# Spline stage of an eight-sublayer decoder on one core: tile scores by TensorE on transposed signs instead of by VectorE and GpSimd row by row

## The reference, cut to what matters

```
xn  = (x - mean) * rsqrt(var + eps) * gamma + beta            # 2048 x 512, second norm of xn0
sig = sign(mean(spline_slopes, -1))                            # 64 tiles x 8 features: each tile owns 8 of the 512
tile_sigs[a, 8a+j] = sig[a, j], zero elsewhere                 # 64 x 512
cluster_sigs = sign(mean of the 8 tile_sigs of a cluster)      # 8 x 512
best_cluster = argmax(sign(xn) @ cluster_sigs.T)
tile = argmax(sign(xn) @ tile_sigs.T inside best_cluster)
x_slice = the 8 features of xn that the chosen tile owns
mn, mx = min and max of x_slice over all tokens that chose this tile
u = clip((x_slice - mn) / (mx - mn + 1e-8), 0, 1 - 1e-6);  gi = int(u * 16)
delta = (bases[tile, j, gi] + slopes[tile, j, gi] * (u*16 - gi)) * output_scale[tile]
out[token, the 8 features of the tile] = delta, zero elsewhere; the sublayer returns xn0 + out
```

## Time and profile before

| | us |
|---|---|
| median of three runs | 1837.11 |
| the profiled execution, its own time | 1835.21 |
| its span in the trace | 1833.4 |
| busy: TensorE / VectorE / ScalarE / GpSimd | 1331.3 / 1511.1 / 869.8 / 556.4 |
| spline phase in the trace, first to last instruction | 620.0 to 767.1 |

### The profile page before, as it was taken

One profiled execution on the slowest core, in us unless ns is written; L12 is line 12 of the kernel. 1 busy time (PEld: TensorE's weight loads), 2 busy tenths in 40 slices (PEclk: granted clock), 3 DMA queues, 4 the chain that ended last, 5 costly groups with the idle time before them and its releaser, 6 DMA issues. The chain is left out here.

```text
span 1833.4 us, 23885 instructions
## 1 busy us (share of the span) xinstructions
PE 1331.3 (73%) x6398; PEld 990.5 (54%) x6398; DVE 1511.1 (82%) x3239; ACT 869.8 (47%) x1726; POOL 556.4 (30%) x573
## 2 busy tenths in 40 slices
PE   4799228886999417444474199069999899998888
PEld 2354114444888303134341188057888788877776
DVE  5999378985877698799759789797899898988885
ACT  3455356662333141154331143136888788843443
POOL 0000005443110141400005013302576666666651
PEclk8999669997999755766585599589999999999999
DMA  5010420000000400155201010223688788888985
GB/s 172 23 35 1 189 75 1 0 0 1 1 1 1 129 23 0 46 162 171 92 0 41 1 46 24 69 51 115 213 242 253 232 245 259 247 249 250 277 238 156
DMA packets 91355, 198.41 MB, mean 108 GB/s; under 512 B 14856, under 2 KB 24200, under 8 KB 90384
## 3 DMA queue, kind: packets, MB, share of 16 engines
q0 software_dynamic: 27120, 91.25, 18.0%
q1 hardware_dynamic: 64160, 106.34, 17.3%
HBM read 181.81 MB, written 15.73 MB: 108 GB/s over the span
## 5 line engine op out<-in xcount | busy, mean ns | idle before, releaser
L2229 POOL DMA_INDIRECT L3f_gd<-rows,idx x160 | 181.0, 1131 | 204.8 <-DVE L3f_gd L2458 180.8
L2229 POOL DMA_INDIRECT L3f_gu<-in_L_ffn_e_up,idx x160 | 167.1, 1045 | 71.3 <-issue 47.2
L2297 PE MATMUL L3f_o_ps<-L3f_euh,L3f_ath 128*128 128x512 f32 x352 | 145.4, 413 | 15.9 <-DVE L3f_atl L2439 15.9
L2285 PE MATMUL L3f_h_ps<-L3f_xh,L3f_edh 128*128 128x512 f32 (+1 forms) x384 | 144.6, 376 | 8.2 <-DVE L3f_xl L2444 8.2
L926 POOL TENSOR_TENSOR L0f_hq<-L0f_hid,magic 128x1408 bf16<-128x1408 f32 x16 | 45.2, 2824 | 338.9 <-DVE L0f_hid L997 338.9
L2285 PE MATMUL L3f_h_ps<-L3f_xl,L3f_edh 128*128 128x512 f32 (+1 forms) x384 | 144.2, 375 | 0.0
L2285 PE MATMUL L3f_h_ps<-L3f_xh,L3f_edl 128*128 128x512 f32 (+1 forms) x384 | 144.2, 375 | 0.0
L2269 PE MATMUL L3f_g_ps<-L3f_oh 128*128 128x128 f32 x704 | 97.5, 283 | 62.7 <-DVE L3f_oh L2426 62.7
L2297 PE MATMUL L3f_o_ps<-L3f_euh,L3f_atl 128*128 128x512 f32 x352 | 137.6, 391 | 0.0
L2297 PE MATMUL L3f_o_ps<-L3f_eul,L3f_ath 128*128 128x512 f32 x352 | 137.5, 391 | 0.0
L2269 PEld LDWEIGHTS L3f_g_ps<-L3f_oh 128*128 128x128 f32 x704 | 91.3, 194 | 73.3 <-issue 68.8
(11 more groups left out here) (526 smaller groups left out, 3702.3 us busy)
## 6 DMA issues: line engine op xcount, KB each, us to landing
L3f_eu<-in_L_ffn_e_up SPq DMA_DIRECT2D x96, 256.0 KB, 4.8
L3f_ed<-in_L_ffn_e_down SPq DMA_DIRECT2D x96, 256.0 KB, 4.5
L2x_ed<-in_L_ffn_e_down SPq DMA_DIRECT2D x32, 256.0 KB, 3.4
rows<-L2x_eo SPq DMA_DIRECT2D x32, 256.0 KB, 2.4
ternary_wgu<-in_L_ffn_w_gate_upT SPq DMA_DIRECT2D x4, 1408.0 KB, 10.4
X<-in_x SPq DMA_DIRECT2D x4, 1024.0 KB, 10.6
L0x_V<-in_ctxT SPq DMA_DIRECT2D x8, 512.0 KB, 3.8
L1f_C<-in_ctx SPq DMA_DIRECT2D x2, 2048.0 KB, 12.6
```

The costliest lines, as they stand in the source:

```text
L2229: pool.indirect_dma_start(buf[j % ND][:, :], None, table, bass.IndirectOffsetOnAxis(ap=idx[:, j:j + 1], axis=0)).then_inc(sem[j % ND], 16)
L2285: last = pe.matmul(h_ps[h][:, 0:cols], lhsT=w[h][:, c, :], rhs=x[:, c, 0:cols], start=(c == 0 and m == 0), stop=(c == DC - 1 and m == 2))
L2297: last = pe.matmul(o_ps[a][:, :], lhsT=w[h][:, a * P:(a + 1) * P], rhs=x[h][:, :], start=False, stop=False)
```

## The change

It touches the spline phase alone.

- **Norm.** VectorE makes `nm = -m * r2`, and ScalarE writes `XN = r2 * x + nm` (no gamma, no beta), 16 activations. VectorE's two instructions per tile are gone.
- **Signs.** TensorE transposes `XN`: per group of four token tiles and per 128 features, four 128 x 128 fp32 transposes into one PSUM buffer of two (`turn`). ScalarE takes the sign from PSUM, with gamma as scale and beta as bias, both now one value per partition, into bf16 (`signs`), one activation of 128 x 512 for each. In ScalarE's list a sign and a norm of the next group alternate.
- **Scores.** A bf16 table `sigs` (feature x 64 tiles, the sign at the owned features) is made by GpSimd (a memset and two `affine_select`) and VectorE (one product). TensorE multiplies the turned signs by it, 4 x 4 matmuls of 64 columns per group, accumulating in PSUM (`score`); those of a group stand in TensorE's list behind the first two turns of the next group.
- **Choice and gather** run in two halves of eight token tiles: the first half needs the scores of groups 0 and 1 only. VectorE reads the scores from PSUM. The gather multiplies `XN`, and its products are written as (feature, tile), so that the writes step over 64 elements and the sums read neighbours.
- **Table.** `TAB` and `LUT` get 16 more columns (273): gamma and beta of the chosen tile. VectorE applies them to `XS` after the gather, so it waits for the whole `LUT` there, ahead of the extremes, and no longer at L1604.
- **Extremes.** The mask is one product-sum (`W1` = ±1e30) and a `min` replaces a product and a sum, for each of two.
- **ScalarE's order.** The 16 moves of the residual: four after the signs, twelve after the `LUT` copies.
- **Gone:** `srow` and its TensorE part, GpSimd's 16 products of signs, VectorE's 16 sums of eight. GpSimd's and VectorE's loops are written out. Two small DMAs come in (gamma and beta into `TAB`), and two 256 KB broadcasts become two strided loads of 2 KB.

The core of the diff:

```diff
@@ gpsimd
-        with pool.Fori(0, NP) as i:
-            for h in range(2):
-                pool.wait_ge(sg_ready, here(i, h))
-                pool.wait_ge(ts_ready, before(i, h))
-                pool.tensor_tensor(sg[h][:, :], sn[h][:, :], srow[:, :], ALU.mult).then_inc(sp_ready, 1)
+        pool.memset(own[:, :, :], 1.0).then_inc(own_made, 1)
...
+        for i in range(NP):
+            pool.wait_ge(oh_made, 1 + 2 * i // NP)
             pool.wait_ge(xs_ready, before(i, 0))
+            pool.tensor_tensor(sg[0][:, :].rearrange("p (b a) -> p a b", b=SL), XN[:, 2 * i, :].rearrange("p (a b) -> p a b", b=SL),
+                               OH[:, 2 * i, :].unsqueeze(2).to_broadcast([P, NTL, SL]), ALU.mult).then_inc(xm_pool, 1)
@@ tensor
+        def turn(g, c):
+            if 4 * g + c >= 2:
+                pe.wait_ge(sgT_ready, 4 * g + c - 1)
+            for j in range(TG4):
+                last = pe.transpose(t_ps[c % 2][:, j, :], XN[:, TG4 * g + j, c * P:(c + 1) * P], ident[:, :])
+            last.then_inc(x_turned, 1)
+        def score(g):
+            pe.wait_ge(sgT_ready, DC * (g + 1))
+            for j in range(TG4):
+                t = TG4 * g + j
+                for c in range(DC):
+                    last = pe.matmul(ts_ps[t // 8][:, t % 8, :], lhsT=sgT[g % 2][:, c, j * P:(j + 1) * P], rhs=sigs[:, c, :],
+                                     start=(c == 0), stop=(c == DC - 1))
+            last.then_inc(scored, 1)
+        for g in range(NT // TG4):
+            pe.wait_ge(xn_ready, TG4 * (g + 1))
+            for c in range(DC):
+                turn(g, c)
+                if g and c == 1:
+                    ...
+                    score(g - 1)
+        score(NT // TG4 - 1)
         for t in range(NT):
+            if t % 8 == 0:
+                pe.wait_ge(oh_made, 1 + t // 8)
             pe.wait_ge(oht_ready, before(i, h))
+            pe.transpose(oh_ps[h], OH[:, t, :], ident[:, :]).then_inc(oh_turned, 1)
@@ scalar
+        act.wait_ge(nm_ready, 1)
+        for t in range(TG4):
+            normalise(t)
+        act.wait_ge(row_in, 32)
+        for g in range(NT // TG4):
+            for c in range(DC):
+                signs(g, c)
+                if g + 1 < NT // TG4:
+                    normalise(TG4 * (g + 1) + c)
+        act.wait_ge(nm_ready, 2)
+        act.wait_ge(xn_ready, NT)
+        for t in range(4):
+            move(t)
@@ vector
+        for k in range(2):
+            s = slice(k * H, (k + 1) * H)
+            dve.wait_ge(scored, 2 * (k + 1))
+            ... (the six instructions of the choice, on the half s)
+            for i in range(k * NP // 2, (k + 1) * NP // 2):
+                dve.wait_ge(xs_ready, before(i, 1))
+                ... (the odd tile's product, and the two sums, reading neighbours)
         dve.wait_ge(xs_ready, 2 * NP + 2)
+        link(dve.tensor_scalar(W1[:, :, :], OH[:, :, :], 2 * BIG, -BIG, ALU.mult, ALU.add))
+        dve.wait_ge(lut_ready, 2 * NP + 2)
+        link(dve.tensor_tensor(XS[:, :, :], XS[:, :, :], LUT[:, :, SC + 1:SC + 1 + SL], ALU.mult))
+        link(dve.tensor_tensor(XS[:, :, :], XS[:, :, :], LUT[:, :, SC + 1 + SL:SC + 1 + 2 * SL], ALU.add))
-            link(dve.tensor_tensor(TS[:, :, :], OH[:, :, :], XM[:, k, :].unsqueeze(2).to_broadcast([P, NT, NTL]), ALU.mult))
-            link(dve.tensor_tensor(TS[:, :, :], TS[:, :, :], W1[:, :, :], ALU.add))
+            link(dve.tensor_tensor(TS[:, :, :], W1[:, :, :], XM[:, k, :].unsqueeze(2).to_broadcast([P, NT, NTL]), ALU.min))
```

More of the change, by code:

```diff
@@ L1316, in spline_phase @@
     BIG = 1e30
-    TW = 2 * SL * GR + 1
+    SC = 2 * SL * GR
+    TW = SC + 1 + 2 * SL
+    TG4 = 4
     m, var, v0, r1, r2, root, w1, w2 = (ph.sb(n, [P, NT]) for n in ("m", "var", "v0", "r1", "r2", "root", "w1", "w2"))
     keep, shift = ph.sb("keep", [P, NT]), ph.sb("shift", [P, NT])
[L1320 to L1323, removed]
+    nm, gT, bT = ph.sb("nm", [P, NT]), ph.sb("gT", [P, DC]), ph.sb("bT", [P, DC])
+    slopes, ss = ph.sb("slopes", [P, DC, GR]), ph.sb("ss", [P, 3, DC])
+    own, sigs = ph.sb("own", [P, DC, NTL]), ph.sb("sigs", [P, DC, NTL], BF16)
+    XN = ph.sb("XN", [P, NT, D])
+    sg, sgT = [ph.sb(f"sg{h}", [P, D]) for h in range(2)], [ph.sb(f"sgT{h}", [P, DC, TG4 * P], BF16) for h in range(2)]
     EXT, RNG = ph.sb("EXT", [NTL, 2]), ph.sb("RNG", [P, NT, 2])
@@ L1454, in _, with normalise, signs, move @@
             act.activation(root[:, :], var[:, :], ACT.Sqrt).then_inc(rooted, 1)
-        with act.Fori(0, NP) as i:
-            for h in range(2):
-                act.wait_ge(xb_ready, here(i, h))
-                act.wait_ge(sp_ready, before(i, h))
-                act.activation(sn[h][:, :], XF[:, 2 * i + h, :], ACT.Sign).then_inc(sg_ready, 1)
-                act.activation(X[:, bass.ds(2 * i + h, 1), :], X[:, bass.ds(2 * i + h, 1), :], ACT.Identity,
-                               scale=keep[:, bass.ds(2 * i + h, 1)], bias=shift[:, bass.ds(2 * i + h, 1)]).then_inc(moved, 1)
+        def normalise(t):
+            act.activation(XN[:, t, :], X[:, t, :], ACT.Identity, scale=r2[:, t:t + 1], bias=nm[:, t:t + 1]).then_inc(xn_ready, 1)
+        def signs(g, c):
+            act.wait_ge(x_turned, DC * g + c + 1)
+            if g >= 2:
+                act.wait_ge(scored, g - 1)
+            act.activation(sgT[g % 2][:, c, :], t_ps[c % 2][:, :, :].rearrange("p t n -> p (t n)"), ACT.Sign,
+                           scale=gT[:, c:c + 1], bias=bT[:, c:c + 1]).then_inc(sgT_ready, 1)
+        def move(t):
+            act.activation(X[:, t, :], X[:, t, :], ACT.Identity, scale=keep[:, t:t + 1], bias=shift[:, t:t + 1]).then_inc(moved, 1)
+        act.wait_ge(nm_ready, 1)
[11 more added lines that the diff above has]
+            move(t)
         act.wait_ge(d_in, 16)
@@ L1466, in _ @@
                 act.wait_ge(oh_turned, here(i, h))
-                act.activation(OHT[:, 2 * i + h, :], oh_ps[h][:, :], ACT.Copy).then_inc(oht_ready, 1)
+                act.activation(OHT[:, 2 * i + h, :], oh_ps[h], ACT.Copy).then_inc(oht_ready, 1)
         with act.Fori(0, NP) as i:
@@ L1470, in _ @@
                 act.wait_ge(l_ready, here(i, h))
-                act.activation(LUT[:, 2 * i + h, :], l_ps[h][:, :], ACT.Copy).then_inc(lut_ready, 1)
+                act.activation(LUT[:, 2 * i + h, :], l_ps[h], ACT.Copy).then_inc(lut_ready, 1)
+        for t in range(4, NT):
+            move(t)
         act.wait_ge(summed, 1)
@@ L1525, in score @@
-        def score(i):
-            for h in range(2):
-                dve.wait_ge(sp_ready, here(i, h))
-                dve.tensor_reduce(TS[:, 2 * i + h, :], sg[h][:, :].rearrange("p (a b) -> p a b", b=SL), AX.X, ALU.add).then_inc(ts_ready, 1)
-        normalise(0)
-        with dve.Fori(0, NP - 1) as i:
-            normalise(i + 1)
-            score(i)
-        score(NP - 1)
-        dve.wait_ge(ts_ready, 2 * NP + 2)
-        dve.wait_ge(io_made, 3)
-        link(dve.tensor_reduce(CS[:, :, :], TS[:, :, :].rearrange("p t (c a) -> p (t c) a", a=SL), AX.X, ALU.add))
@@ L1546, in _ @@
[L1546 to L1557 removed]
+        dve.wait_ge(own_made, 3)
```

108 lines of the change are left out of this document (44 added, 64 removed).

## The result

The changed kernel takes 1813.92 us (median of 4 runs, 1811.12 to 1821.21) against 1836.34 us for the kernel before (median of 4 runs, 1835.55 to 1837.71): a ratio of 0.9883, 95% interval 0.9866 to 0.99. The prediction was 1813.1 us, range 1804 to 1821. The profiled execution took 1814.82 us with a span of 1813.1. That the median lies 0.8 us from the forecast is in part luck: the stretch that was changed gained 26.0 us where 24 were taken, and the rest of the kernel, which the change leaves alone, gave some of it back (see the end of the experiments).

The account below looks back on a forecast made before the run. VectorE was taken to bound scoring, then gather and table values side by side. The phase's gain, 25.8 us at full clock or 22.0 at half, was taken as 24: 1837.1 - 24 = 1813.1 us, range 1804 to 1821.

Parts of the forecast that it names:

- full-clock numbers: Spline phase with TensorE at 2.4 GHz through scoring: all scored at 653.7, gain 25.8 us.
- Scoring: Signs and norms on ScalarE and TensorE: ScalarE-bound groups of 5.6 us at full clock, all scored at 653.7 or 660.1.
- half-clock case: TensorE at 1.2 GHz through scoring: middle groups last 7.9 us, all scored at 660.1, gain 22.0 us.
- Choice and gather: VectorE's halves of eight tiles: choice 3.8 us, gather pair 2.54 us, four pairs 10.8 us, strided writes free.
- Table values: Table products behind all transposes: 16.1 us at granted clock 0.50; VectorE waits 9 us for `LUT`.
- Behind it: VectorE's work from whole `LUT` to `DL`: 32.1 us, down from 34.7.
- Rival 1: Gather: strided writes cost what strided reads do, 0.39 us more per product, pair 3.3 us; gain 21, 1816 us; 22%.
- Rival 2: Table products run at full clock, about 8 us; gather and table end near 676; gain 32, 1805 us; 12%.
- Rival 3: Scoring: ScalarE's signs take 1.0 us each from start to start; gain 20, 1817 us; 10%.
- Rival 4: Gather: products with a step of 64 elements far dearer, kernel slower than before; 1844 us at four times; 3%.
- two chains run side by side, and shortening one alone gives about 1 us: Kernel before, from the one-hot on: gather 24.4 us, table values 23.3 us, ends 1.1 us apart.
- if the phases behind change by more than 1 us: Sign for the phases after the spline phase: a change above 1 us would make the prediction wrong all the way.

Follow-up runs that it names:

- e3: Changed kernel with one-hots and table padded by 64 rows of zeros, so table products use 128 rows: 1808.57 us, phase 1.61 us less.
- e1: Changed kernel with the gather's products written as before, sums reading every eighth element: 1810.05 us, phase 1.07 us more.
- e5: Kernel before with only the gather's new layout: 1839.64 us beside 1840.66 for the kernel before, phase 2.15 us less.
- e2: Changed kernel with one choice over all 16 tiles after the last score, instead of two halves: 1814.19 us, phase 2.52 us more.
- e4: Changed kernel with small products for gamma and beta ahead of the large ones, the large ones split nine and seven: 1806.59 us, phase 6.83 us less.
- e7: e4 with the zero padding of e3, extremes padded too, 12 large products ahead of the extremes instead of nine: 1805.37 us, ratio 0.9803 to the kernel before.
- e6: Kernel before with half of its gather left out, the other chosen inputs set to 0.5: 1828.9 us, phase 11.66 us less.

## Why the prediction was right, step by step

The forecast's mechanism held, and at its full-clock numbers, though the clock was full only in parts:

```
step                       predicted (full / half clock)   measured
group 0 done               635.4                           635.3
first half scored          644.1 / 647.4                   643.9
first one-hot              647.9 / 651.2                   647.8
all scored                 653.7 / 660.1                   654.5
second one-hot             662.5 / 665.8                   662.7
gather ends                673.3 / 676.6                   673.8
LUT whole                  682.6 / 686.5                   682.2
DL                         714.8 / 718.7                   714.5
gain of the phase          25.8 / 22.0                     26.0
```

- *Scoring.* Signs and norms alternate 1.37 to 1.38 us apart, predicted 1.40. The granted clock was 0.50 to 0.66, so this was nearer the half-clock case, but that case was mis-sized: the 16 score matmuls were put at 1.9 us, the upper bound from 128 columns, and took 1.06 at a granted clock of 0.50 (635.31 to 638.20). The third sign of a group starts 3.9 us into it and waits for nothing (639.22, from 635.31), where the third turn was to hold it until 5.1. What was left to the clock was the stretch behind 642.11, ahead of the first half's scores: faster in the changed kernel, at 0.50 in e3, which scored its first half 1.0 us later by it. The forecast had 3.3 us between its two clocks there; taking the middle, 24, gave away 2 us.
- *Choice and gather.* A choice takes 3.84 us (3.8 predicted), four pairs with their ends 11.0 (10.8), a pair 2.64 (2.54). That the pair came out is luck, two errors that nearly cancel. The prediction took the whole 0.38 us of the cheaper sum off the 2.92 of the kernel before and set the strided writes to nothing. The runs give the layout only 0.11 of it in the changed kernel (2.75 in e1 to 2.64) and 0.23 in the kernel before (2.92 to 2.69, e5), so within a pair the writes cost 0.27 and 0.15. The other 0.17, from 2.92 to 2.75, came with the rest of the change to the gather (loops written out, `XN` in place of `XF`), which the prediction doesn't have and no run takes apart.
- *Table values.* This was the step that carried the forecast. 16.2 us from 665.98 to the last copy's end at 682.22 (16.1 predicted), at 0.50; VectorE waited 7.84 us (9). e2 and e4 show it from both sides: delaying the gather by 9.4 us costs 2.5, taking the table out of VectorE's way gains 6.8.
- *Behind it.* 32.2 us from `LUT` to `DL`, 32.1 predicted.
- *Rival 1* (writes cost as reads for both engines: a pair 3.3 us). Refuted by the 2.64 and by GpSimd's unchanged 1.08. The Trainium skill ("Advanced Engine Details and Errata", Memory Cachelines) has the penalty without a difference between engines. For VectorE's writes the trace agrees (+0.36); for GpSimd's it doesn't show.
- *Rival 2* (table products at full clock). Refuted as it stood: 0.50 for 16 us, though TensorE had worked before. e3 and e7 reach 1.00 in these products with other operands.
- *Rival 3* (signs at 1.0 us). Refuted: 0.77 each, 0.68 from start to start (629.66 to 630.34). *Rival 4* (slower): no.
- *Wrong: the two chains of the kernel before.* The prediction read "two chains run side by side, and shortening one alone gives about 1 us" from two ends that lie 1.1 us apart. But in the kernel before VectorE needs `LUT` only at 730.04, when it reaches the spline's grid cells, and the extremes' turns need a free TensorE only at 716.20:

```profile
716.20 0.64 PE L1421 MATMUL L1f_mm_ps<-ident,L1f_MM 128*64 128x128 f32 x2 [11.96 <-DVEq L1567]
...
730.04 2.29 DVE L1604 TENSOR_TENSOR L1f_KW<-L1f_KN,L1f_LUT 128x2048 f32<-128x2048 f32 x1
```

  The table had 11 us to spare. e6 gained 11.66 us by the gather alone, which used up nearly all of it (TensorE idled 0.32 us ahead of the turn, not 11.96), e5 gained 2.15. The change itself made the table urgent: gamma and beta now come through `LUT`, ahead of the extremes. The sum was right because it followed the changed order; the sentence on the kernel before was not, and it would have discouraged the cheapest edits.
- *Wrong: "if the phases behind change by more than 1 us".* They did, by 5.8 us in the first profile (488.95 + 582.76 against 490.38 + 575.54), and by this sign the prediction would have been wrong all the way, while its chain in the changed phase held step by step. A bound of 1 us on a stretch that scatters by 11 can't test anything. The gap between the phase's 26.0 us and the 22.4 us of the medians lies within this scatter.

## What to carry to other kernels

Two chains that end at the same time are not both urgent: look for the first instruction that reads each result. When a value is moved into a shared table, its reader inherits the table's whole chain; here a small product for the early readers, ahead of the large ones, gave back 6.8 us. Compare the changed stretch, not only the whole time, when another part of the kernel scatters by several us.

## What the runs showed of the hardware

- The same 32 table passes were at a granted clock of 0.50 throughout with 64 rows of operands (TensorE busy 15.68 of 16 us in the changed kernel, 8.00 of 8 in e4) and reached 1.00 with 128 rows, half of them zeros (e3, e7). With 128 rows the products of 16 columns were at 0.50 (TensorE busy 7.44 of 8 us), and in those of 2 columns the clock fell from 1.00 to 0.50 with TensorE busy throughout (e7).
- A GpSimd memset of 64x2048, which reads nothing, held a 16-element tensor_scalar of VectorE until it was done (0.17 us became 1.50, from 621.95 to 623.45; the memset ended at 623.42, e3). An instruction with two inputs just ahead of it, at 621.74, was not held (0.17 us). The Trainium skill ("SBUF — State Buffer", SBUF: two separate sides) has the two engines' shared port as an exclusive lock for the whole instruction; the trace agrees.
- A product of 512 elements written with a step of 64 fp32 elements takes VectorE 1.05 us against 0.69; GpSimd's takes 1.08 to 1.09 against 1.07 to 1.08 (e1).
